# Spreading VectorE's dependent gate steps between the larger operations of two token pairs, in the first layer's feed-forward of a two-layer tower

## What is computed

```python
gate = softmax(relu(x @ Wg1 + bg1) @ Wg2 + bg2)          # 3 experts
top_w, top_i = top_k(gate, 2); top_w = softmax(top_w)
q, k = (x @ Wqk + bqk) split, each as 3 experts of 64
for e in 0..2:
    ve = x @ Wv[e] + bv[e]
    if e == 0: qe = conv1d(qe, conv_w, width 3) + conv_b
    att = softmax(masked(qe @ ke.T / 8))                  # rows see only earlier tokens
    ys.append(att @ ve)
out = (ys * w_e).reshape(...) @ Wp + bp                   # w_e: the top-2 weights, 0 elsewhere
```

## Time and profile before

| | |
|---|---|
| median of 3 runs | 1969.83 us (1968.5 to 1972.9) |
| profiled execution, time | 1969.73 us |
| profiled execution, span of its core | 1968.1 us |
| VectorE busy over the span | 1289.9 us (66%) |
| TensorE matmul busy over the span | 1551.7 us (79%) |
| ScalarE busy over the span | 961.6 us (49%) |
| the stage that is changed | about 448 to 684 us of the span |

### The profile page before, as it was taken

How to read it: one execution, slowest core, us unless ns; L and a number is a source line. 1 busy time by engine, 2 the same in 40 slices (tenths; PEclk the granted TensorE clock), 3 DMA queues, 4 the chain that set the end, 5 groups by cost and what they waited for, 6 DMA issues and landing times.

```text
span 1968.1 us, 37567 instructions
## 1 busy us (share of the span) xinstructions
PE 1551.7 (79%) x13020; PEld 1205.5 (61%) x13020; DVE 1289.9 (66%) x4233; ACT 961.6 (49%) x2769; POOL 481.7 (24%) x689
## 2 busy tenths in 40 slices
PE   0076764888888758888888877999999949999996
PEld 0032221776666546666666656777777738888885
DVE  7898885787888767877877744666666642222221
ACT  1275999873545445554454423444444414444442
POOL 7401333000000012222222211222222223333332
PEclk9985555559999869999999988999999969999998
DMA  3000000119991000000000000000000038778785
GB/s 74 18 1 1 1 1 1 22 42 172 183 174 11 0 1 1 0 0 0 0 0 0 0 10 18 26 25 24 24 24 24 25 89 199 190 193 199 189 197 137
DMA packets 136263, 113.02 MB, mean 57 GB/s; under 512 B 29416, under 2 KB 128456, under 8 KB 136136
## 3 DMA queue, kind: packets, MB, share of 16 engines
q1 hardware_dynamic: 119320, 91.70, 20.3%
q0 software_dynamic: 16864, 20.33, 5.4%
HBM read 69.19 MB, written 45.94 MB: 59 GB/s over the span
## 4 chain that ended last, share of the span: by engine, by line
PE 46%; DVE 34%; ACT 12%; issue 4%; POOL 2%; DVEq 0%; DMA 0%; ACTq 0%; POOLq 0%; SPq 0%
ACT bank L716 9%; PE bank L2374 8%; PE bank L2364 6%; PE bank L1007 5%; PE bank L2359 3%; PE bank L1000 3%; PE bank L2030 2%; PE bank L1690 2%; DVE R L1577 2%; DVE WK L1577 2%; DVE R L1882 2%; PE bank L966 1%; PE bank L640 1%; PE bank L641 1%; PE bank L1718 1%
## 5 line engine op out<-in xcount | busy, mean ns | idle before, releaser
L1047 POOL TENSOR_TENSOR WK<-WK,mhalf 128x2 f32<-128x2 f32 (+1 forms) x96 | 78.7, 819 | 546.0 <-DVE WK L1024 247.1
L2411 ACT ACTIVATE R<-bank,R 128x256 f32<-128x256 f32 x234 | 98.5, 472 | 187.1 <-PE bank L2364 185.5
L716 ACT ACTIVATE bank<-bank,nbias,sc 128x128 f32<-128x128 f32 x384 | 168.9, 952 | 21.6 <-POOL nbias L528 21.6
L2291 POOL DMA_INDIRECT moe_sum<-WK x78 | 121.5, 1558 | 229.0 <-DMA moe_sum<-WK 166.2
L2262 DVE SCALAR_TENSOR_TENSOR WK<-bank,R,WK 128x192 f32<-128x192 f32 x78 | 28.9, 412 | 207.6 <-PE bank L2374 207.6
L716 ACT ACTIVATION_READ_ACCUMULATOR bank<-bank,nbias,sc 128x1 f32 x384 | 162.1, 726 | 0.0
L2374 PE MATMUL bank<-R 128*128 128x192 f32 x936 | 158.6, 326 | 0.0
L1007 PE MATMUL bank<-WK,R 96*128 96x256 f32 x576 | 147.5, 398 | 6.2 <-ACT WK L973 3.5
L2374 PEld LDWEIGHTS bank<-R 128*128 128x128 f32 x936 | 151.3, 190 | 0.1
L1007 PEld LDWEIGHTS bank<-WK,R 96*128 96x128 f32 x576 | 106.2, 194 | 25.9 <-ACT WK L973 6.6
L2364 PE MATMUL bank<-R 128*128 128x256 f32 x468 | 113.0, 392 | 0.0
(11 more groups left out here) (507 smaller groups left out, 4131.3 us busy)
## 6 DMA issues: line engine op xcount, KB each, us to landing
moe_rows_in<-zeros SPq DMA_DIRECT2D x1, 25026.0 KB, 147.2
R<-in_L_ffn_w SPq DMA_DIRECT2D x39, 576.0 KB, 5.0
R<-in_L_ffn_w SPq DMA_DIRECT2D x39, 384.0 KB, 3.1
R<-moe_rows_in SPq DMA_DIRECT2D x39, 194.0 KB, 4.6
R<-in_L_ffn_w SPq DMA_DIRECT2D x78, 96.0 KB, 3.7
R<-in_L_ffn_b SPq DMA_DIRECT2D x39, 96.0 KB, 5.1
moe_sum<-resid POOLq DMA_DIRECT2D x16, 192.0 KB
moe_sum<-WK POOLq DMA_INDIRECT x78, 5.9
```

Of the source, the lines that this page charges most:

```text
L716: ins = nc.scalar.activation(s, s, ACT.Exp, bias=nbias[:, u, k:k + 1], scale=col(SS), accum_out=units(sum_all, g, u)[:, k:k + 1])
L1047: nc.gpsimd.tensor_tensor(a.rs[:, 0:n], a.ve[:, 0:n], mhalf[:, 0:n], ALU.pow).then_inc(f.root, 1)
L2291: pool.indirect_dma_start(out=acc, out_offset=bass.IndirectOffsetOnAxis(ap=x_id[k % B3][:, t:t + 1].bitcast(U32), axis=0), in_=x_y[k % B3] ...
L2411: ins = nc.scalar.activation(x_hid[q], hidden_at(p, n), ACT.Gelu, bias=xb_1[h][:, q:q + 1])
```

## The change

`Chain` gets `mark` (let the operation raise the semaphore and return the count) and `wait` (wait for a count), so that the wait of a dependent step can stand later than its producer. VectorE's order in this stage is then written anew:

- the first part has more yields: statistics / aggregate / epsilon / normalise / convolution, v, relu and logits / maximum / subtraction; the second part: sum / reciprocal / product, comparisons and two choices / everything up to the scaling / first projection / first residual / the second sequence's two. So segments 1 and 2 of the list above are interleaved one by one, and segments 5 and 6 as well;
- within the convolution, the addition of v and the relu go between its three steps;
- the last steps of the choice and the four steps of the gate weights go between the masked scores and the row maxima. With them `v.wait_ge(f.gate_exp, per(g, 2, 2))` moves from behind both row maxima to a place in front of the first one;
- the factor `a.ff` (two small operations per half) is dropped; the six scalings take two per-partition scalars (1/row sum and gate weight) with two multiplications instead of one;
- `vector_l_tables`, which runs beside the last second part, yields three times first, so that it stays at its place.

No DMA, and nothing of TensorE, ScalarE or POOL, is changed. The core of the diff:

```diff
@@ -50,6 +50,14 @@
         self.k += 1
         ins.then_inc(self.sem, 1)
         self.eng.wait_ge(self.sem, self.k)
+
+    def mark(self, ins):
+        self.k += 1
+        ins.then_inc(self.sem, 1)
+        return self.k
+
+    def wait(self, k):
+        self.eng.wait_ge(self.sem, k)
 
     def clear(self):
         self.eng.sem_clear(self.sem)
@@ -1126,7 +1134,17 @@
 
         def vector_f_1(v, ch, g, a, f):
 
-            variances(v, ch, a, f, tiles_of(g, a))
+            for i in range(M):
+                ins = nc.vector.bn_stats(a.st[:, i, :], tiles_of(g, a)[:, i, :])
+            stats = ch.mark(ins)
+            yield
+            ch.wait(stats)
+            for i in range(M):
+                ins = nc.vector.bn_aggr(a.mv[:, i, :], a.st[:, i, :])
+            means = ch.mark(ins)
+            yield
+            ch.wait(means)
+            nc.vector.tensor_scalar(a.ve[:, 0:M], a.mv[:, :, 1], 1e-5, None, ALU.add).then_inc(f.var, 1)
             yield
             normalised(v, a, f, tiles_of(g, a), a.x, per(g, 1, 1)).then_inc(f.x, 1)
             yield
@@ -1134,71 +1152,106 @@
             v.wait_ge(f.qk, per(g, 3, 1))
             q0 = a.qkT[0:HE, 0, :].rearrange("p (t n) -> p t n", t=M)
             qc = a.qc[0:HE, :].rearrange("p (t n) -> p t n", t=M)
-            ch.step(nc.vector.tensor_scalar(qc, q0, f_conv[0:HE, 1:2], f_convb[0:HE, 0:1], ALU.mult, ALU.add))
-            ch.step(nc.vector.scalar_tensor_tensor(out=qc[:, :, 1:P], in0=q0[:, :, 0:P - 1], scalar=f_conv[0:HE, 0:1],
-                                                   in1=qc[:, :, 1:P], op0=ALU.mult, op1=ALU.add))
-            nc.vector.scalar_tensor_tensor(out=qc[:, :, 0:P - 1], in0=q0[:, :, 1:P], scalar=f_conv[0:HE, 2:3],
-                                           in1=qc[:, :, 0:P - 1], op0=ALU.mult, op1=ALU.add).then_inc(f.conv, 1)
+            middle = ch.mark(nc.vector.tensor_scalar(qc, q0, f_conv[0:HE, 1:2], f_convb[0:HE, 0:1], ALU.mult, ALU.add))
             v.wait_ge(f.v_p, per(g, 1, 1))
             nc.vector.tensor_tensor(a.vv, a.bank[2][:, 0:M * VG].rearrange("p (t n) -> p t n", t=M),
                                     fb_vg.unsqueeze(1).to_broadcast([P, M, VG]), ALU.add).then_inc(f.v, 1)
+            ch.wait(middle)
+            left = ch.mark(nc.vector.scalar_tensor_tensor(out=qc[:, :, 1:P], in0=q0[:, :, 0:P - 1], scalar=f_conv[0:HE, 0:1],
+                                                          in1=qc[:, :, 1:P], op0=ALU.mult, op1=ALU.add))
             v.wait_ge(f.v, per(g, 1, 1))
-            ch.step(nc.vector.tensor_scalar(a.vv[:, :, D:VG], a.vv[:, :, D:VG], 0.0, None, ALU.max))
+            relu = ch.mark(nc.vector.tensor_scalar(a.vv[:, :, D:VG], a.vv[:, :, D:VG], 0.0, None, ALU.max))
+            ch.wait(left)
+            nc.vector.scalar_tensor_tensor(out=qc[:, :, 0:P - 1], in0=q0[:, :, 1:P], scalar=f_conv[0:HE, 2:3],
+                                           in1=qc[:, :, 0:P - 1], op0=ALU.mult, op1=ALU.add).then_inc(f.conv, 1)
+            ch.wait(relu)
             for i in range(M):
                 ins = nc.vector.tensor_tensor(a.gp[:, i], a.vv[:, i, D:VG].unsqueeze(1).to_broadcast([P, TE, GH]),
                                               fw_g2.rearrange("p (n e) -> p e n", e=TE), ALU.mult)
             ch.step(ins)
             ch.step(nc.vector.tensor_reduce(a.gt, a.gp, X, ALU.add))
-            ch.step(nc.vector.tensor_tensor(a.gt, a.gt, fb_g2.unsqueeze(1).to_broadcast([P, M, TE]), ALU.add))
-            ch.step(nc.vector.tensor_reduce(a.m4, a.gt, X, ALU.max))
+            logits = ch.mark(nc.vector.tensor_tensor(a.gt, a.gt, fb_g2.unsqueeze(1).to_broadcast([P, M, TE]), ALU.add))
+            yield
+            ch.wait(logits)
+            top = ch.mark(nc.vector.tensor_reduce(a.m4, a.gt, X, ALU.max))
+            yield
+            ch.wait(top)
             nc.vector.tensor_tensor(a.gt, a.gt, over_e(a.m4), ALU.subtract).then_inc(f.gate_in, 1)
 
         def vector_f_2(v, ch, g, a, f):
 
             v.wait_ge(f.gate_exp, per(g, 2, 1))
-            ch.step(nc.vector.tensor_reduce(a.m4, a.ge, X, ALU.add))
-            ch.step(nc.vector.reciprocal(a.m4, a.m4))
+            whole = ch.mark(nc.vector.tensor_reduce(a.m4, a.ge, X, ALU.add))
+            yield
+            ch.wait(whole)
+            share = ch.mark(nc.vector.reciprocal(a.m4, a.m4))
+            yield
+            ch.wait(share)
             nc.vector.tensor_tensor(a.gt, a.ge, over_e(a.m4), ALU.mult).then_inc(f.gate_in, 1)
             v.wait_ge(f.gate_in, per(g, 2, 2))
             for n, (a0, a1) in enumerate(((0, 1), (0, 2), (1, 2))):
                 ins = nc.vector.tensor_tensor(a.cmp[:, n, :], a.gt[:, :, a0], a.gt[:, :, a1], ALU.is_ge)
             ch.step(ins)
-            ch.step(nc.vector.tensor_tensor(a.we[:, :, 0], a.cmp[:, 0, :], a.cmp[:, 1, :], ALU.max))
-            ch.step(nc.vector.tensor_scalar(a.cmp[:, 0:2, :], a.cmp[:, 0:2, :], -1.0, 1.0, ALU.mult, ALU.add))
-            nc.vector.tensor_tensor(a.we[:, :, 1], a.cmp[:, 0, :], a.cmp[:, 2, :], ALU.max)
-            ch.step(nc.vector.tensor_scalar(a.m4, a.cmp[:, 2, :], -1.0, 1.0, ALU.mult, ALU.add))
-            ch.step(nc.vector.tensor_tensor(a.we[:, :, 2], a.cmp[:, 1, :], a.m4, ALU.max))
-            yield
-
-            for i in range(M):
-                v.wait_ge(f.scores, per(g, M, i + 1))
-                for b, at in (((0, slice(0, 3, 2)), (1, slice(1, 2))), ((2, slice(0, 1)), (3, slice(1, 3))))[i]:
-                    n = 2 if at in (slice(0, 3, 2), slice(1, 3)) else 1
-                    ins = nc.vector.scalar_tensor_tensor(
-                        out=a.s[:, i, at, :], in0=a.bank[b][:, 0:n * P].rearrange("p (e n) -> p e n", e=n),
-                        scalar=HE ** -0.5, in1=f_mask.unsqueeze(1).to_broadcast([P, n, P]), op0=ALU.mult, op1=ALU.add)
-                ch.step(ins)
+            nc.vector.tensor_tensor(a.we[:, :, 0], a.cmp[:, 0, :], a.cmp[:, 1, :], ALU.max)
+            less = ch.mark(nc.vector.tensor_scalar(a.ff[:, 0:2, 0:2], a.cmp[:, 0:2, :], -1.0, 1.0, ALU.mult, ALU.add))
+            yield
+
+            def scaled_scores(i, b, at):
+
+                n = 2 if at in (slice(0, 3, 2), slice(1, 3)) else 1
+                return nc.vector.scalar_tensor_tensor(
+                    out=a.s[:, i, at, :], in0=a.bank[b][:, 0:n * P].rearrange("p (e n) -> p e n", e=n),
+                    scalar=HE ** -0.5, in1=f_mask.unsqueeze(1).to_broadcast([P, n, P]), op0=ALU.mult, op1=ALU.add)
+
+            def row_tops_of(i):
+
                 nc.vector.tensor_reduce(a.nm[:, i, :], a.s[:, i], X, ALU.max, negate=True).then_inc(f.rowmax, 1)
+
+            ch.wait(less)
+            nc.vector.tensor_tensor(a.we[:, :, 1], a.ff[:, 0, 0:2], a.cmp[:, 2, :], ALU.max)
+            last = ch.mark(nc.vector.tensor_scalar(a.m4, a.cmp[:, 2, :], -1.0, 1.0, ALU.mult, ALU.add))
+            v.wait_ge(f.scores, per(g, M, 1))
+            scaled_scores(0, 0, slice(0, 3, 2))
+            ch.wait(last)
+            picked = ch.mark(nc.vector.tensor_tensor(a.we[:, :, 2], a.ff[:, 1, 0:2], a.m4, ALU.max))
+            masked = ch.mark(scaled_scores(0, 1, slice(1, 2)))
+            ch.wait(picked)
             v.wait_ge(f.gate_exp, per(g, 2, 2))
-            ch.step(nc.vector.tensor_tensor(a.we, a.we, a.ge, ALU.mult))
-            ch.step(nc.vector.tensor_reduce(a.m4, a.we, X, ALU.add))
-            ch.step(nc.vector.reciprocal(a.m4, a.m4))
-            ch.step(nc.vector.tensor_tensor(a.we, a.we, over_e(a.m4), ALU.mult))
+            kept = ch.mark(nc.vector.tensor_tensor(a.we, a.we, a.ge, ALU.mult))
+            ch.wait(masked)
+            row_tops_of(0)
+            v.wait_ge(f.scores, per(g, M, 2))
+            scaled_scores(1, 2, slice(0, 1))
+            ch.wait(kept)
+            total = ch.mark(nc.vector.tensor_reduce(a.m4, a.we, X, ALU.add))
+            masked = ch.mark(scaled_scores(1, 3, slice(1, 3)))
+            ch.wait(total)
+            part = ch.mark(nc.vector.reciprocal(a.m4, a.m4))
+            ch.wait(masked)
+            row_tops_of(1)
+            ch.wait(part)
+            weights = ch.mark(nc.vector.tensor_tensor(a.we, a.we, over_e(a.m4), ALU.mult))
             for i in range(M):
                 v.wait_ge(f.exp, per(g, M, i + 1))
                 ch.step(nc.vector.reciprocal(a.rsum[:, i, :], a.rsum[:, i, :]))
-                ch.step(nc.vector.tensor_tensor(a.ff[:, i, :], a.rsum[:, i, :], a.we[:, i, :], ALU.mult))
+                if i == 0:
+                    ch.wait(weights)
                 for e in range(TE):
-                    ins = nc.vector.tensor_scalar(a.s[:, i, e, :], a.s[:, i, e, :], a.ff[:, i, e:e + 1], None, ALU.mult)
+                    ins = nc.vector.tensor_scalar(a.s[:, i, e, :], a.s[:, i, e, :], a.rsum[:, i, e:e + 1], a.we[:, i, e:e + 1],
+                                                  ALU.mult, ALU.mult)
                 ins.then_inc(f.scaled, 1)
             yield
 
-            for i in range(M):
```

(18 more changed lines are left out.)

## The result

The changed kernel is slower: 1980.31 us in the median of its runs (1977.14 to 1981.9) against 1972.87 for the kernel before, measured beside it (1968.5 to 1973.87). The ratio is 1.0042, with a 95% interval of 1.0029 to 1.0055, so 5.7 to 10.9 us more. Forecast were 1.4 us more, 1971.1 in a range up to 1976.5. The direction and the mechanism were right, the size was not, and the time lies outside the range. About 3 of the 9.2 us between forecast and median are not the change's: the forecast was counted from 1969.83 us, the first median of the kernel before, which became 1972.87 with two more runs.

What follows compares the result with a forecast made beforehand. VectorE was taken to lead, with TensorE close behind. Fourteen halves of 14.21 us less 196.65 gave +2.3, start -1.2, end +0.3: +1.4 us on 1969.73, thus 1971.1 us, range 1966.5 to 1976.5.

Steps and rivals of the forecast that it cites:

- What bounds before: Stage of the kernel before: VectorE leads, TensorE 0.17 and 0.56 us behind; 14.05 us per half on average.
- The step that decides: Gate exponential's wait before the first row maxima: exponentials from 2.07 instead of 1.27 us after the turn, halves 14.21 us.
- The wait for POOL: VectorE's normalisation, started earlier, would newly wait 0.2 to 0.3 us for POOL's power.
- Two scalars per scaling: VectorE's scalings: 0.06 us more each for the second scalar, three taking 0.85 us instead of 0.68.
- Rival 3: Scalings: second scalar costs 0.1 us more each than taken, 4.2 us in all, 1975.3 us; chance 0.10.
- Dependence costs 0.12 us: VectorE's small steps: covering a dependent step with independent work saves about 0.12 us.
- rival 2: VectorE's stream gets no shorter by interleaving, marked independent operations being drained like dependent ones; 1978.7 us; chance 0.07.
- From the second transposes to the next turn is TensorE's own way, 8.54 us: Last part of each half: TensorE with ScalarE's copies takes 8.54 us, added to 5.67 for a 14.21 us interval.
- that idle time: Sign that the forecast is right: TensorE's first probability transposes (L1256) wait longer than 0.81 us.
- Start: Stage start to first turn: 0.59 + 0.17 + 0.45 = 1.21 us earlier, 0.45 of it from the logits' steps.
- End: After the last turn: last scores come 0.50 us later, 0.23 is won back, +0.27 us.
- Rival 1: Gate exponential does not hold the row maxima: halves of 13.38 us, 1958.5 us in all; chance 0.09.

Runs made afterwards that it cites:

- e5: The kernel before, with only ScalarE's second gate exponential moved in front of the copy of the turned tokens; ratio 1.0005 to the kernel before.
- e1: The changed kernel with the gate exponential's wait and the four gate-weight steps put back behind both row maxima; ratio 0.9953, 1966.42 us.
- e4: The changed kernel with ScalarE's second gate exponential issued in front of the copy of the turned tokens; ratio 0.9936 to the kernel before, 1962.1 us.
- e7: e4 with two instead of five idle matmuls in front of the turn; ratio 0.9909 to the kernel before, 1956.92 us.
- e6: e4 with the dropped factor put back: product with the gate weight, then scalings with one scalar each; ratio 0.9947 to the kernel before.
- e8: e4 without the interleaving of the two pairs (statistics, gate, last steps of logits and output each in one piece); ratio 0.9954 to the kernel before.
- e3: The changed kernel with four added identity matmuls filling TensorE's idle time before the first transposes; ratio 1.0029 to the kernel before.
- e10: The changed kernel with two instead of five idle matmuls in front of the turn; ratio 0.9992 to the kernel before.
- e2: The kernel before, with only the gate exponential's wait moved in front of the first row maxima; ratio 1.0170, 2009.04 us.
- e9: e4 with no idle matmuls in front of the turn instead of five; ratio 0.9907 to the kernel before.
- e12: The changed kernel with four instead of five idle matmuls in front of the turn; run once, 1983.82 us beside 1973.53 for the kernel before.

## Why the prediction was right and wrong, point by point

**What bounds before: right.** e5 shows that ScalarE's order does not hold the kernel before, and e1, which changes VectorE's order alone, brings the halves from 14.05 to 13.40 us: VectorE was in the lead. e4 and e7 show TensorE close behind, at 13.30.

**The step that decides: right.** The wait for the gate exponential in front of the first row maxima holds the loop; the trace has every station of the sum. From the turn: L1220 at 1.43 (forecast 1.41), exponentials 2.09 (2.07), first transposes 4.51 (4.48), second 5.69 (5.67). From there to the next turn 8.60 against 8.54. The half is 14.30 instead of 14.21, and 14 x 0.09 = 1.3 us is the size of that miss. Two thirds of it, 0.06, lie in TensorE's own way from the second transposes to the next turn, which the forecast took over from the kernel before; the stations account for 0.02. The one in front of L1220 is 0.10 us (537.40 + 0.20 to 537.70), where I had taken 0.04. The wait for POOL, 0.2 to 0.3 us in the forecast, is not to be seen: the normalisation starts at 534.50, 0.98 after the epsilon (1.08 where I read it) and 0.11 behind the end of the gate's last step, so it came at 1.92 us and not at 2.0 to 2.1. It changed nothing, for the normalisation is not on the loop any more.

**Two scalars per scaling: right.** Three take 0.86 us (forecast 0.85), and e6 prices the exchange at 0.02 us per half. Rival 3 is out.

**Dependence costs 0.12 us: right.** Reduction, aggregate and reciprocal of different chains start 0.12 to 0.16 us apart in the rows above, where dependent ones alone start 0.19 to 0.20 apart, and L1208 starts 0.08 after L1220, of which it is independent (537.70, 537.78); so rival 2 is out. By the eight copies of the Trainium skill (VectorE: DVE Perf Modes, The DRAIN you can't avoid) the order of waits would be without effect on VectorE's time. The trace does not agree, and e8 against e5, with two small operations fewer per half, has halves that are 0.77 us shorter, after which TensorE leads. The prediction passed over that the same section of the Trainium skill also says that a next operation which is not held starts earlier; with that the 0.08 us agree.

**"From the second transposes to the next turn is TensorE's own way, 8.54 us": wrong in four halves of fourteen.** This term took TensorE's clock as 1.00, from the earlier trace rows, for a kernel in which TensorE idles 1.34 us in one piece. The prediction itself named that idle time as a sign, and put no price on it. In four halves the clock fell behind it, 4 x 1.47 = 5.9 us. That is the largest part of the miss between the two profiled executions; in the medians, where e3 is only 0.13% below the changed kernel, its size is not shown. What the runs show in place of the term: 8.60 us at a granted clock of 1.00; in the long half shown, 9.15 (527.12 to 536.27), and another 0.93 lost in front of it, for the second transposes come 6.62 us after the turn instead of 5.69. e3, with the idle time filled, has no fall, and 5.9 us are gone from its halves. e10 had none either, with the idle time left as it was, so e3 alone would not show the cause; the rows of the four falls do, in which the clock is 0.50 and the same instructions take 0.8 instead of 0.55 us.

**Start: mis-sized.** Forecast -1.2, measured -0.2. The forecast had the logits' steps end 0.45 us earlier, with the convolution under v. It did not work out: with nothing else beside it, VectorE waits for TensorE's product of v (L1277, 2.00 us), and two steps of the convolution, which stood in front of v before, are now queued behind that wait. The steps ended at 460.04 instead of 459.39, counted from the stage's start 11.6 us instead of 11.1. Part of the wait is TensorE's clock, but not all: where the products of v ran at the full clock in both orders, the memset behind these steps comes 9.65 us after the stage's start in the old order (e2) and 9.88 in the new one (e4). So the new order costs 0.2 us there instead of saving 0.45. How long TensorE stays at the lower clock at the start of the stage differs from run to run: the first turn comes 14.89 us after the stage's start here, 14.21 in e4, 17.52 in e3, 15.97 in e9. That makes the start's sum in one pair of executions a matter of chance in part.

**End: mis-sized.** Forecast +0.3, measured +1.6. After 3.54 us of idle time the transposes, products and projection of the last pair run at the lower clock; L1309 takes 0.90 twice, and VectorE waits 2.53 and 1.05 us for the projections. In the kernel before these two waits were 2.03 and 0.22 us. There the clock also fell, behind 4.05 us of idle time, but it came back during the projections. In e5, which has the same order of VectorE, it did not, and the same stretch took 24.83 us instead of 23.48. So most of this miss need not come from the change.

Sum in the profiled execution: 1.4 forecast, + 1.3 + 5.9 + 1.0 + 1.3 = 10.9, against 10.8 measured in the stage. Most of it is TensorE's clock, and the parts of start and end are in part luck of this pair of executions.

**Rival 1** was the case to repair the kernel for. It took two `yield`s on ScalarE, and a third for the stage behind.

## What to carry to other kernels

When a wait is moved up in an in-order queue, follow its signal back through the *other* engine's queue: what stands in front of the producer there becomes part of your loop, whether or not it has to do with the data. Spread dependent small steps only to places where their own inputs are already there, and check what is queued behind each wait. And if the sum leaves TensorE idle for a microsecond or more at one place in each round, put the lower clock into the range: it can cost more than the wait.

## What the runs showed of the hardware that was not expected

TensorE's granted clock can fall from 2.4 to 1.2 GHz behind an idle time of 1.34 us in an otherwise busy stage (busy 143.29 of 168.00 us), for some 3.4 us, at a price of 1.47 us per fall in the changed kernel; one fall in e12 lasted some 17 us and cost 7.1. It does so in some rounds only: four, none, one and two of fourteen in one execution each of kernels that differ by a few idle matmuls elsewhere. With idle times of 0.37 to 0.81 us at that place it did not happen behind the first half, also not where TensorE had least to do (e9). A wait of 1.78 us (e2) brought it in nine halves of fourteen. What selects the rounds stays open.
